# GpSimd waits for VectorE's normalised rows before it clears a back lane's packed buffers

## The reference

```
x = x + diag_attention(layernorm(x))          # one head, only the diagonal of the softmax
x = x + local_transformer(layernorm(x))       # 2 layers: 8 heads, windows of 64, then LN and a gated MLP
x = x + causal_attention(layernorm(x))        # 16 heads of width 8
x = x + mixture_of_experts(layernorm(x))      # softmax gate, top 2 of 8 experts, plus a shared one
```

## Time and profile before

| | |
|---|---|
| median of 3 runs | 1790.74 us (1790.58 to 1791.3) |
| the profiled execution | 1798.88 us, span of its records 1797.0 us |
| PE busy | 1562.0 us, 87% |
| DVE busy | 1229.1 us, 68% |
| ACT busy | 949.2 us, 53% |
| POOL busy | 597.3 us, 33%, 401 instructions |
| chain that ended last | PE 56%, DVE 20%, ACT 13%, DMA 5%, issue 3%, POOL 1% |

### The profile page before, as it was taken

How to read it: one execution, slowest core, us unless ns; L and a number is a source line. 1 busy time by engine, 2 the same in 40 slices (tenths; PEclk the granted TensorE clock), 3 DMA queues, 4 the chain that set the end, 5 groups by cost and what they waited for, 6 DMA issues and landing times.

```text
span 1797.0 us, 29686 instructions
## 1 busy us (share of the span) xinstructions
PE 1562.0 (87%) x11632; PEld 919.2 (51%) x11632; DVE 1229.1 (68%) x2636; ACT 949.2 (53%) x1771; POOL 597.3 (33%) x401
## 2 busy tenths in 40 slices
PE   5689976899978999889998989889998889788988
PEld 2354543556454555545555455555555446545555
DVE  5867769765677667785588865876678557764634
ACT  3476753476443764438645566448643554552441
POOL 1856636161060612615034430616115115110000
PEclk9899998999989999999999999999998999988999
DMA  3201001310061001501014101411015002403102
GB/s 125 68 1 28 22 1 38 55 23 25 27 109 26 23 24 36 124 1 29 27 47 104 29 2 36 104 39 23 24 36 124 3 10 74 96 28 80 47 1 65
DMA packets 37291, 80.12 MB, mean 45 GB/s; under 512 B 6782, under 2 KB 22654, under 8 KB 33776
## 3 DMA queue, kind: packets, MB, share of 16 engines
q1 hardware_dynamic: 37152, 78.22, 18.0%
HBM read 54.74 MB, written 8.78 MB: 35 GB/s over the span
## 4 chain that ended last, share of the span: by engine, by line
PE 56%; DVE 20%; ACT 13%; DMA 5%; issue 3%; SPq 1%; POOL 1%; POOLq 0%; DVEq 0%; ACTq 0%
PE ps L507 51%; PE ps L512 5%; ACT bigs L1025 4%; ACT work L943 3%; DVE bsmall L1316 3%; DMA pqs<-scr_partsb 2%; DMA scr_partsb<-bigs 2%; DVE fsmall L1198 1%; DMA v2s<-vs 1%; DVE fsmall L1190 1%; DVE work L1161 1%; DVE work L1160 1%; ACT L977 1%; SPq L1596 1%; DVE fxn L1106 1%
## 5 line engine op out<-in xcount | busy, mean ns | idle before, releaser
L1445 POOL TENSOR_TENSOR fsmall<-fsmall,consts 128x8 f32<-128x8 f32 (+1 forms) x140 | 201.2, 1447 | 276.2 <-DVE fsmall L1100 265.9
L507 PE MATMUL ps<-bxt,mw 128*128 128x512 f32 x504 | 249.9, 609 | 8.4 <-ACT bigs L1051 4.5
L507 PE MATMUL ps<-maskb,identb 128*128 128x128 bf16 (+1 forms) x1152 | 234.8, 246 | 15.5 <-ACT work L943 11.8
L1468 POOL TENSOR_TENSOR work<-work 128x1024 f32<-128x1024 f32 x56 | 133.0, 2376 | 310.9 <-DVE work L1161 310.8
L1316 DVE TENSOR_REDUCE bsmall<-ps 128x1 f32<-128x512 f32 (+3 forms) x308 | 178.2, 632 | 38.5 <-PE ps L507 37.8
L943 ACT ACTIVATE work<-ps,fsmall 128x128 f32<-128x128 f32 x448 | 164.2, 514 | 57.4 <-DVE fsmall L1202 57.4
L507 PE MATMUL ps<-wqkv,h 128*128 128x512 f32 x336 | 165.0, 623 | 18.4 <-ACT vs L903 9.1
L1499 POOL TENSOR_TENSOR work<-work,fsmall 128x1024 f32<-128x1024 f32 x56 | 106.2, 1897 | 185.7 <-DVE fsmall L1193 185.7
L1025 ACT ACTIVATE bigs<-ps 128x512 f32<-128x512 f32 x280 | 148.2, 659 | 12.4 <-PE ps L507 11.7
L512 PE MATMUL ps<-ident,work 128*128 128x128 f32 x924 | 133.9, 287 | 20.3 <-ACT work L943 12.0
L507 PE MATMUL ps<-pks,pqs 96*128 96x128 bf16 (+3 forms) x448 | 109.5, 313 | 44.6 <-DMA pqs<-scr_partsb 24.9
(11 more groups left out here) (335 smaller groups left out, 2979.9 us busy)
## 6 DMA issues: line engine op xcount, KB each, us to landing
mw<-in_experts SPq DMA_DIRECT2D x63, 384.0 KB, 3.1
pks<-scr_partsb SPq DMA_DIRECT2D x42, 192.0 KB
pqs<-scr_partsb SPq DMA_DIRECT2D x126, 64.0 KB
v2s<-vs SPq DMA_DIRECT2D x14, 512.0 KB, 4.4
v2s<-vs SPq DMA_DIRECT2D x14, 384.0 KB, 5.7
scr_partsb<-bigs SPq DMA_DIRECT2D x7, 768.0 KB, 5.3
wqkv<-in_experts SPq DMA_DIRECT2D x9, 384.0 KB, 3.1
xin<-in_x SPq DMA_DIRECT2D x7, 256.0 KB, 3.5
```

The lines of the kernel that those rows point to most:

```text
L507: return nc.tensor.matmul(o, a, b, start=start, stop=stop, skip_group_check=True)
L1445: return nc.gpsimd.tensor_tensor(out, x, consts[:, k:k + 1].broadcast_to([x.shape[0], x.shape[1]]), op)
L1468: nc.gpsimd.tensor_tensor(R.qk[:, m, :], R.qk[:, m, :], R.part[m % 2], ALU.add).then_inc(R.l_add.sem, 1)
```

## The change

One line is added to `back_constants`, ahead of the memsets. It is called twice in the program, at the first back of each lane. `R.b_xn` is the signal of VectorE's four TENSOR_SCALARs. No instruction's place in its queue changes, and VectorE, TensorE, ScalarE and SyncE have the same programs as before.

```diff
             def back_constants(R):
+                pool.wait_ge(R.b_xn.sem, R.b_xn.at(0, 1))
                 for r in range(2):
                     i = nc.gpsimd.memset(R.pq_words[r], 0.0)
                 i.then_inc(R.q_cleared, 1)
                 nc.gpsimd.memset(R.va[:, :, :, CD + 1:32], 0.0)
                 nc.gpsimd.memset(R.va[:, :, :, CD:CD + 1], 1.0).then_inc(R.back_ready, 1)
```

## The result

The change makes the kernel faster: 1785.33 us against 1794.41 us for the kernel before (medians of 20 runs each), ratio 0.9949 with a 95% interval of 0.9933 to 0.9965. That is 9.1 us of 1794 (6.3 to 12.0 by the interval) where 8.5 were forecast. The three runs shown before the prediction had a median of 1790.74 us; over the 20 runs here the same kernel has 1788 to 1799 us, so only the ratio of runs made together counts, and one profile's span (1797.0 before, 1787.3 after) says little: from one execution to the next it moves by as much as the change is worth.

A forecast was written before the change was run, and what follows sets the result against it. The chain was taken to pay for VectorE's normalisation being held off by GpSimd's clears at both entries. Gains 4.5 + 4.0 = 8.5 us off the median: 1790.74 - 8.5 = 1782.2 us, range 1780.4 to 1787.0.

The forecast's parts named there:

- The stall and its cause: At both entries GpSimd's clears hold off VectorE's normalisation, 5.62 and 5.02 us instead of 1.11; the wait frees it.
- The sum: Gains of both entries added: 4.5 + 4.0 = 8.5 us, with bounds 7.5 and 8.6 us.
- The clears beside VectorE's memsets: After the normalisation, GpSimd's delayed clears run beside VectorE's memsets of clear_packed_k; this overlap was costed at nothing.
- the stall changes its place: Rival, chance 0.10: the clears hold a long VectorE memset instead; 1.7 us slower than before, 1792.4 us.
- GpSimd 1.9 us late: First entry: clears, key normalisations and roots queued behind GpSimd's wait come 1.9 us later; 0 lost, bound 0.5 us.
- The cast beside the roots: First entry; rival, chance 0.05: VectorE's cast and subtraction each held by one L1445 root, losing 3.2 us, 1785.4 us.
- TensorE's clock: Second entry: with its 3.48 us idle stretch gone, TensorE was expected to go on at 2.4 GHz instead of 1.2.
- The 4.0 us pass whole: Second entry: the packed transfers still decide TensorE's wait, so the full 4.0 us gain passes that wait.
- TensorE's low clock after that wait (0.50) is in the time already: Second entry, behind TensorE's wait for the packed transfers: its low clock was taken as already included in the time.
- more than forecast: Rival, chance 0.04: TensorE's better clock at either entry brings 1 or 2 us more.
- Both gains reach the end: Both entries' gains, 4.5 and 4.0 us, reach the end; the rival losing one, chance 0.13, said about 1786.5 us.
- the stated range: The forecast's overall range, 1780.4 to 1787.0 us, taking in the rival that loses one gain.

The follow-up runs named there:

- e4: Kernel before with the wait placed between GpSimd's two 128x2048 memsets, so only the first runs into the normalisation: ratio 0.9968 (0.995 to 0.9985).
- e3: Kernel before, no wait, the normalisation at both entries written as SCALAR_TENSOR_TENSOR instead of TENSOR_SCALAR: ratio 0.9942 (0.9919 to 0.9964).
- e7: As e3, without the wait, and at the second entry GpSimd instead of VectorE clears the packed keys: ratio to before 0.9939 (0.9917 to 0.996).
- e1: Kernel before with the wait added at the first entry alone: ratio 0.9976 (0.9957 to 0.9994), 4.3 us.
- e2: Kernel before with the wait added at the second entry alone: ratio 0.998 (0.9963 to 0.9997), 3.6 us.
- e8: As e7, and at the first entry ScalarE clears packed keys by two activations, leaving VectorE two memsets: ratio to before 0.9953 (0.9932 to 0.9975).

## Why the prediction was right

*The stall and its cause.* Right. The sum said 4.51 us at the first entry and 4.0 at the second; to the step that the prediction looked at they are 4.52 and 4.09 us in the profiles, and by times 4.3 and 3.6 us, with intervals of about 3 us to each side. That the clears are the cause is shown by taking half of them away (e4) and by a form that they don't hold (e3). At the first entry not all of the 5.62 us was theirs: the third TENSOR_SCALAR started behind the last memset and still took 1.05 us, beside the key normalisation L1479, where in the profile after none takes over 0.34. So some 0.7 of the 4.5 us were bought from that instruction, which now runs beside VectorE's memsets.

```profile
291.66 1.05 DVE L1106 TENSOR_SCALAR bxn<-x,bsmall 128x128 f32<-128x128 f32 x1
```

*The clears beside VectorE's memsets.* Costed at nothing from one pair of short memsets; right, all at 1.76 and 1.8 us. The row bore less than the text put on it: it compared the length of one short memset (0.27 us for 256 columns) with the distance between the starts of long ones, whose own 1.76 us are 0.86 ns a column. The rival that the stall changes its place had no ground here. e7 shows how it would have looked had a cast stood there instead of a memset.

*GpSimd 1.9 us late.* The bound of 0.5 us was not reached: TensorE waited 0.30 us and nobody behind it did.

*The cast beside the roots.* The row was right for L1445: in the profile after, the cast and the subtraction behind it lie beside it and take 0.68 and 1.22 us. GpSimd's memsets do exclude casts (e7), so the rule of the Trainium skill that the prediction cites holds for them; VectorE's cast, started later, was not blocked to the end of these small roots. The roots paid a little themselves: the four that took 6.43 us before take 7.39 us beside the casts and the subtraction, which the sum had not counted. It cost nothing, since the last is wanted late. Four rows of GpSimd's timeline after, all four and then the first, third and fourth alone:

```profile
297.02 7.39 POOL L1446 TENSOR_TENSOR fsmall<-fsmall,consts 128x8 f32<-128x8 f32 x4
297.02 2.03 POOL L1446 TENSOR_TENSOR fsmall<-fsmall,consts 128x8 f32<-128x8 f32 x1
300.47 1.63 POOL L1446 TENSOR_TENSOR fsmall<-fsmall,consts 128x8 f32<-128x8 f32 x1
302.07 2.34 POOL L1446 TENSOR_TENSOR fsmall<-fsmall,consts 128x8 f32<-128x8 f32 x1
```

With the usual 1.63 us the first would have ended within the cast at 298.33 us and the fourth just after the next cast began (303.69 to 304.37 us); both end 0.04 us behind that cast. The second begins within the first cast and takes 1.88 us, the fourth begins within the subtraction. The third only ends within the subtraction and is not longer, and the cast of the earlier trace rows lay wholly inside its root (1.65 us). So it looks as if such a root collides with them at its beginning, and with a cast at its end, and not in between; no run was made to test that.

*TensorE's clock.* It stayed at 2.4 GHz at the second entry as forecast. TensorE reached the wait 6.31 us sooner after the normalisation (25.88 instead of 32.19 us) where the sum asked for at least 3.5, and the transfers took what went beyond 4.09, as forecast: the wait grew from 3.77 to 5.99 us.

*What the sum left out.* "The 4.0 us pass whole" is too small for the second entry, since "TensorE's low clock after that wait (0.50) is in the time already" took that term as fixed. It shrank: part of the low stretch now falls into the longer wait, and to the end of the span the second entry is worth 6.1 us in this pair of profiles. That is the 1 or 2 us of the rival "more than forecast", chance 0.04, for which the prediction took the transfers to cover TensorE's clock; they cover what comes before the wait and not what comes behind it.

*Both gains reach the end.* By e1 and e2 each does in part; by the profiles the second does and grows, and the first is still about whole 350 us on. Whether all of it is left at the end is not shown. Something of it is: e1's interval leaves out nothing, if only just, and the change, e3, e7 and e8 lie 8.4 to 11.0 us below before by their ratios, where the second entry alone would give 6.1 to 6.6. In the profiled executions the distance between before and after wanders between the entries (5.0 us ahead at 323 us, 3.6 at 1588); executions of one kernel differ there by as much.

*The sum.* 8.5 us forecast, 9.1 measured with 6.3 to 12.0 as interval. With 6.1 for the second entry it would have been 10.6, which the interval takes in too, so the good agreement of the total is partly luck and does not confirm the 4.0. The absolute 1782.2 us was too low by 3 us, since the three runs it started from lay below the median of more; 1785.33 us lies in the stated range but not in the narrower one of the forecast itself, 1781.2 to 1783.6.

## What to carry to other kernels

When an instruction takes many times what its twins elsewhere take, look at what the other engine on the same memory does in just that time: here a few idle microseconds of the engine with time to spare bought 4.5 on the path at one entry and 6 at the other. A wait is one cure; writing the instruction in a form that does not collide does as well and delays nobody. Cutting the colliding work into pieces is no cure if the other engine comes in between them only by chance. Whoever moves clears to another engine should look at what they will run beside there. And a gain should be followed past the next wait: the wait may swallow it, or, as here, TensorE's slow stretch may move into the wait and add to it.

## What the runs showed of the hardware

- A held TENSOR_SCALAR is not always let in at the end of the GpSimd instruction that runs. Before, at the first entry, it outlasted all four memsets (4.32 us for the first of the four TENSOR_SCALARs); at the second it came in behind two (3.54 us), and e7's cast came in between two (2.27 us, while the second of these memsets took 2.35 instead of 1.80). With sixteen short memsets a run of clears was either entered early (1.18 and 1.28 us for four) or not at all (6.08 to 6.20 us), and the same program did both.
- VectorE's memsets, and a SCALAR_TENSOR_TENSOR with both inputs in SBUF, ran beside GpSimd's memsets at full speed. The TENSOR_SCALAR (5.0 to 5.6 instead of 1.1 us for four) and the fp32 to bf16 cast (2.27 instead of 0.68 us) did not.
- GpSimd's L1445, a power of 128x8 numbers that lasts 1.6 us, held no cast of 0.68 us, whether it lay inside or over one end. The three in the profile after that began within a cast or the subtraction, or whose end fell on a cast, took 1.88 to 2.34 us; the one that only ended within the subtraction kept 1.63.
- TensorE was granted 0.50 from about 1628 to 1633 us behind a wait of 3.77 us, all of it in work. Around a wait of 5.99 us 0.50 was there 3 us before the work began, and 1.00 was back within 4 us of the wait's end. The longer wait made the work behind it 1.25 us shorter.
